# A pipeline over the routed part's tiles, and a slot table of row numbers, in a graph layer with a mixture of experts

## The chip, the cores and the metric

The kernel runs on one core of a Trainium2 chip. The metric is the device time of one execution in microseconds; lower is better. Three runs of the kernel before took 1408.47, 1411.64 and 1416.46 us, median 1411.64. All other times here come from one profiled execution. Its span, from the first to the last instruction, is 1334.0 us.

## The reference, cut to what matters

```python
# x: 3125 nodes x 256; 50000 edges; D = 256, F = 1024, E = 8 experts, K = 2 of them for each node
x = x + gnn(layernorm(x), ...)        # gather h[src], weights from edge features, segment sum over dst
xn = layernorm(x)
shared = gelu(xn @ W1s + b1s) @ W2s + b2s
topw, topi = top_k(softmax(xn @ Wr), 2); topw = topw / sum(topw)
# routed, for each node n and each of its two experts e, with its weight w:
routed[n] += w * (gelu(xn[n] @ W1p[e] + b1p[e]) @ W2p[e] + b2p[e])
x = x + shared + routed
```

All is fp32. Products are made from halves: an operand is rounded to a high part, the remainder is the low part, and three matmuls (high-high, high-low, low-high) stand for one.

## The kernel before, in words

The program is a chain of blocks; at the end of each all engines meet.

*Node and edge blocks* (0 to 684 us). The edge block goes through 98 steps of 512 edges. GpSimd gathers the rows `h[src]` by four indirect DMAs a step (line 552), VectorE makes the edge products, TensorE sums them by one-hot matrices. On the side SP fills a table `slots_d` in HBM with blank rows of 258 words (line 522): 256 features, a node number and a weight.

*Update block* (684 to 779 us). It finishes the nodes, writes the new rows `xnew_d`, their layernorm `xn_d` and its columns `xT_d` to HBM, and computes the router's logits.

*Shared block* (779 to 924 us). Five groups of 640 nodes go through the shared expert. A group is 16 half blocks "up" (6 matmuls of 320 columns each, then Gelu on ScalarE, `hhi` on ScalarE, `hlo` on VectorE) and five "down" of 24 matmuls. During group 0 VectorE computes the routing: each node has two places (`pos_i`) in the slot table, where every expert owns whole tiles of 256 slots, three at least. `counts_i` holds each expert's number of tiles and its first tile. Then GpSimd writes rows to the table: SP loads the normalized rows of a group twice (line 1371), GpSimd puts node number and weight beside them and scatters 128 rows of 1032 bytes at a time (line 1448), 50 scatters. SP waits for these buffers in the same queue in which it loads the columns of the next group and stores the output.

*Routed block* (924 to 1334 us). Expert after expert, tile after tile; here there are 29 tiles. A tile s goes so:

- SP loads the tile's 256 rows of the slot table to `x_slot_tile` (line 1713) once VectorE has taken the node numbers and weights of the tile before (`meta_done`).
- TensorE turns them (`turn`, line 1871) into `psX`, in the middle of the down blocks of the tile before. ScalarE copies them to `xf`, VectorE makes `xhi` and `xlo` (lines 1802, 1804).
- TensorE does eight up blocks (`q_psA`, line 1293: 6 matmuls of 256 columns), ScalarE the Gelu (line 1763), VectorE `high` and `low` (lines 1811, 1815).
- TensorE then does eight down blocks (`q_psB`, line 1300: two halves of 3 matmuls), each waiting for its `hlo`.
- VectorE's output, after all its `low` of the tile: for each half of 128 slots the node number to `index`, `biased` (line 1834), `ob` (line 1837). It waits for `ob_free`.
- GpSimd adds `ob` to the rows of the output by an indirect DMA that adds (line 1739), waits until it has landed, frees `ob`, and only then issues the next: two additions a tile.

`index` and `ob` have one buffer for each half. Weights of the next expert are split into high and low parts in eight pieces of 512 columns (ScalarE line 1785, VectorE line 1852) during the first two tiles of an expert, four in each, and then SP loads the two matrices of a later expert (1024 KB each, lines 1259 and 1261) to `x_raw`. The experts are three times two in a loop and two behind it; tiles beyond an expert's second are a loop of their own (`further`).

## Time and profile before

| | |
|---|---|
| median of three runs | 1411.64 us |
| span of the profiled execution | 1334.0 us |
| its own time | the page gives none beside the span; the median above is 77.6 us more than the span |
| TensorE busy | 1217.9 us, 91% |
| VectorE busy | 1029.3 us, 77% |
| ScalarE busy | 826.6 us, 62% |
| GpSimd busy | 720.3 us, 54% |
| mean granted TensorE clock | 0.955 |

The page names engines so: PE is TensorE's matmuls, PEld its weight loads, DVE is VectorE, ACT ScalarE, POOL GpSimd, SP SyncE; a "q" behind the name is the engine's queue of other instructions. Times are from the span's start. The granted clock is 1.00 at the full 2.4 GHz. Matmuls overlap in the record, so that their rate is read from one start to the next. The busy share of a whole execution mixes stages with different limits: VectorE and TensorE are both nearly full in the edge stage, while in the routed stage VectorE works 254 of 410 us.

### The profile page before, as it was taken

What the parts mean: (1) busy time and instruction counts of PE and PEld (TensorE: products, weight loads), DVE (VectorE), ACT (ScalarE), POOL (GpSimd) and SP (SyncE); (2) the same over time, 40 slices, a digit from 0 to 9 for tenths busy, and PEclk for the clock granted to TensorE, in tenths of its full rate; (3) what the DMA queues carried; (4) which work ended last, traced back from release to release, by engine and by line L of the source; (5) the groups of instructions that cost most, each with busy time, mean ns of one, the idle gap of its engine ahead of it and who ended that gap; (6) DMA issues with size and microseconds to landing.
All of it is one profiled execution on the core that took longest, in us unless ns stands there. A gap on an engine that the chain in (4) does not pass through costs nothing. (4 is left out here: it accounts for less than half of the span.)

```text
span 1334.0 us, 32063 instructions
## 1 busy us (share of the span) xinstructions
PE 1217.9 (91%) x8631; PEld 1120.6 (84%) x8632; DVE 1029.3 (77%) x2584; ACT 826.6 (62%) x2362; POOL 720.3 (54%) x823
## 2 busy tenths in 40 slices
PE   2789999999999999999989899998998997989995
PEld 2578888888888888888887679998998997989995
DVE  7589999999999999999856866444765674666663
ACT  2688888888888888888834674453442443343431
POOL 7178888788887888878731104651242232233332
PEclk9989999999999999999975979999999998999998
DMA  6443444344344444434543474764324334332232
GB/s 241 155 131 111 120 117 119 111 119 120 111 122 120 115 116 118 121 110 118 171 126 116 163 259 131 251 216 140 99 44 103 78 62 99 95 95 46 46 49 28
DMA packets 107219, 160.47 MB, mean 120 GB/s; under 512 B 16414, under 2 KB 82750, under 8 KB 106656
## 3 DMA queue, kind: packets, MB, share of 16 engines
q1 hardware_dynamic: 73680, 90.86, 21.4%
q0 software_dynamic: 29568, 65.62, 20.6%
q10 hardware_dynamic: 3920, 3.41, 0.8%
q8 instruction: 19, 0.31, 0.1%
q14 instruction: 32, 0.26, 0.1%
HBM read 110.99 MB, written 48.85 MB: 120 GB/s over the span
## 5 line engine op out<-in xcount | busy, mean ns | idle before, releaser
L576 ACT ACTIVATE hots<-hot,sh_st 128x128 f32<-128x128 f32 x1568 | 467.9, 390 | 3.8 <-PE psY L743 3.3
L552 POOL DMA_INDIRECT rows<-h_tab,src_st x392 | 404.9, 1033 | 117.2 <-issue 116.9
L743 PEld LDWEIGHTS psY<-prod,hots 128*128 128x128 f32 x2352 | 324.6, 192 | 20.4
L743 PE MATMUL psY<-prod,hots 128*128 128x128 f32 x2352 | 326.1, 275 | 0.0
L1739 POOL DMA_INDIRECT out_rows<-q_ob,q_index x58 | 125.5, 2163 | 294.4 <-DVE q_ob L1837 193.3
L740 PE MATMUL psY<-prod,hots 128*128 128x256 f32 x784 | 234.4, 381 | 0.6 <-DVE prod L636 0.6
L636 DVE TENSOR_TENSOR prod<-psW,rows 128x384 f32<-128x384 f32 x392 | 213.8, 545 | 0.0
L1763 ACT ACTIVATE q_hf<-q_psA,q_b 128x256 f32<-128x256 f32 x232 | 109.7, 473 | 111.7 <-PE q_psA L1293 109.0
L1300 PE MATMUL q_psB<-x_whi,q_hhi 128*128 128x256 f32 x464 | 138.7, 299 | 24.5 <-DVE q_hlo L1815 24.5
L651 DVE TENSOR_TENSOR y_sb<-y_sb,psY 64x512 f32 x196 | 133.4, 681 | 10.2 <-issue 5.7
L1293 PE MATMUL q_psA<-q_xhi,x_whi 128*128 128x256 f32 x464 | 133.2, 287 | 4.0 <-DVE q_xlo L1804 2.8
L1300 PE MATMUL q_psB<-x_wlo,q_hhi 128*128 128x256 f32 x464 | 133.7, 288 | 0.0
L1300 PE MATMUL q_psB<-x_whi,q_hlo 128*128 128x256 f32 x464 | 133.7, 288 | 0.0
L1293 PE MATMUL q_psA<-q_xlo,x_whi 128*128 128x256 f32 x464 | 131.5, 283 | 0.0
L1293 PE MATMUL q_psA<-q_xhi,x_wlo 128*128 128x256 f32 x464 | 131.5, 283 | 0.0
L728 PE MATMUL psW<-w1hi,cols_hi 128*128 128x256 f32 x392 | 108.2, 309 | 16.2 <-DVE cols_hi L621 6.5
L740 PEld LDWEIGHTS psY<-prod,hots 128*128 128x128 f32 x784 | 119.4, 191 | 0.8 <-DVE prod L636 0.8
L634 DVE TENSOR_TENSOR prod<-psW,rows 128x128 f32<-128x128 f32 x392 | 110.5, 282 | 5.4 <-DMA rows<-h_tab,src_st 1.8
L1300 PEld LDWEIGHTS q_psB<-x_whi,q_hhi 128*128 128x128 f32 x464 | 90.6, 195 | 28.0 <-issue 27.0
L566 ACT ACTIVATE hid<-psE 128x512 f32<-128x512 f32 x98 | 58.7, 598 | 89.2 <-PE psE L720 87.6
L728 PEld LDWEIGHTS psW<-w1hi,cols_hi 128*128 128x128 f32 x392 | 75.0, 191 | 45.8 <-issue 45.1
L729 PE MATMUL psW<-w1lo,cols_hi 128*128 128x256 f32 x392 | 98.0, 283 | 0.0
(213 smaller groups left out, 2509.6 us busy)
## 6 DMA issues: line engine op xcount, KB each, us to landing
x_raw<-in_w SPq DMA_DIRECT2D x18, 1024.0 KB, 8.0
slots_d<-blank SPq DMA_DIRECT2D x49, 258.0 KB
x_slot_tile<-slots_d SPq DMA_DIRECT2D x30, 258.0 KB, 2.8
s_row<-xn_d SPq DMA_DIRECT2D x50, 128.0 KB, 3.1
cols_lo<-ele_split SPq DMA_DIRECT2D x196, 32.0 KB
rows<-h_tab,src_st POOLq DMA_INDIRECT x392, 2.8
x_sb<-in_x SPq DMA_DIRECT2D x5, 640.0 KB, 5.8
h_tab<-x_sb ACTq DMA_DIRECT2D x5, 640.0 KB, 3.3
```

Of the source, the lines that this page charges most:

```text
L552: pool.indirect_dma_start(out=rows[p][:, c, :, :].rearrange("p a u -> p (a u)"), out_offset=None, in_=h_tab, in_offset=bass.IndirectOffset ...
L576: ins = nc.scalar.activation(hots[p][:, 4 * c + k, :], hot[p][:, c, :], ACT.Copy, scale=sh_st[p][:, 4 * c + k:4 * c + k + 1])
L634: nc.vector.tensor_tensor(slots[:, 0::7, :], w[:, 0:2, :], rows[p][:, c, 0:1, :].to_broadcast([P, 2, MUL]), ALU.mult)
L636: nc.vector.tensor_tensor(slots[:, 1:7, :].rearrange("p (b k) u -> p b k u", b=2), w[:, 2:4, :].unsqueeze(2).to_broadcast([P, 2, 3, MUL]), ...
L651: ins = nc.vector.tensor_tensor(acc, acc, psY[p][lo:lo + HALF, :], ALU.add)
L728: nc.tensor.matmul(o, hidT[p][:, P * c:P * c + P], w1hi[:], start=True, stop=False)
L740: ins = nc.tensor.matmul(y[:, 1::2, :], hots[p][:, 4 * c, :], a[:, 4:8, :], start=(c == 0), stop=(c == C - 1), skip_group_check=True)
L743: ins = nc.tensor.matmul(y[:, 2 * k::6 - 2 * k, :][:, 0:2, :], hots[p][:, 4 * c + k + 1, :], a[:, 0::k + 1, :][:, 0:2, :], start=False, st ...
L1293: ins = nc.tensor.matmul(ps, w1_part(w, k, f), x(k), start=(n == 0), stop=(n == len(terms) - 1))
L1300: ins = nc.tensor.matmul(ps, h, w2_part(w, f), start=(f == 0 and n == 0), stop=(f == FC - 1 and n == 2))
L1739: pool.indirect_dma_start(out=out, out_offset=bass.IndirectOffsetOnAxis(ap=index[m][:], axis=0), in_=ob[m][:], in_offset=None, compute_op= ...
L1763: nc.scalar.activation(hf[f][:], psA[f % 4][:, 0:TOK], ACT.Gelu, bias=b1_st[:, f:f + 1]).then_inc(gelu_done, 1)
```

## The change

- *Slot table.* It holds only node number and weight (8 bytes), 94 places for each partition, so that one DMA loads all of it to SBUF (`meta_all`). It is blanked by one DMA; the 49 of the edge loop go. `place` gives the positions in that layout and works on both experts at once.
- *Shared block.* No row loads. The 50 scatters write `meta_i` straight to the table, and each waits (`turn_of`) for an up or down block of TensorE in groups 1 to 4. After the last GpSimd waits for all, loads the table and gathers the rows of tile 0 from `xn_d`.
- *Rows of a tile* are now gathered by GpSimd (`gather_rows`: two index copies, two indirect DMAs of 128 rows), into one buffer, as soon as TensorE has turned the tile before.
- *TensorE* interleaves the down blocks of tile s-1 with the up blocks of tile s: down f, up f; the transpositions of s+1 follow up block 1. A tile's down has one of two sides of `psB`, `xhi` and `xlo` have two sides. ScalarE writes `xhi` from PSUM; `xf` and VectorE's cast are gone.
- *VectorE's output* in tile s is that of tile s-2, after the first `low`; `xlo` of s+1 follows the third. *GpSimd* in one loop: rows of tile d+4, free `ob` half 1 of tile d-1 when its addition has landed, addition of half 0 of tile d, wait for it, addition of half 1.
- *Weights.* W1 and W2 of an expert are split in separate tiles (W2 in its own first tile, W1 of the next expert in the second) and loaded apart. The loop over experts is written out; copies of the biases are gone.

```diff
+def gather_rows(nc, pool, v, s):
+    for m in range(SUB):
+        ins = pool.tensor_copy(index[:, m:m + 1], meta_all[:, at(s), m, 0:1].rearrange("p o c -> p (o c)"))
+    ins.then_inc(v["index_set"], 1)
+    pool.wait_ge(v["index_set"], s + 1)
+    pool.sem_inc(v["gather_go"], 1)
+    for m in range(SUB):
+        pool.indirect_dma_start(
+            out=rows[:, m, :], out_offset=None, in_=v["xn_d"],
+            in_offset=bass.IndirectOffsetOnAxis(ap=index[:, m:m + 1], axis=0)).then_inc(v["rows_in"], 16)
...
+            def turn_of(n):
+                g, r = 1 + n // (FC + GROUP), n % (FC + GROUP)
+                if r <= FC:
+                    pool.wait_ge(up_done, g * UP + min(2 * r + 1, UP))
+                else:
+                    pool.wait_ge(down_done, g * GROUP + r - FC + GROUP)
...
+            for t in range(NT):
+                g = t // GROUP
+                if t % GROUP == 0 and g > 1:
+                    pool.wait_ge(sent[g % 2], 32 * GROUP * (g // 2))
+                for k in range(2):
+                    turn_of(2 * t + k)
+                    pool.sem_inc(send_go, 1)
+                    pool.indirect_dma_start(
+                        out=slots_d, out_offset=bass.IndirectOffsetOnAxis(ap=pos_i[:, t, k:k + 1], axis=0),
+                        in_=meta_i[:, t, k, :], in_offset=None).then_inc(sent[g % 2], 16)
+            pool.wait_ge(sent[0], 32 * GROUP * ((NG + 1) // 2))
+            pool.wait_ge(sent[1], 32 * GROUP * (NG // 2))
+            pool.dma_start(meta_all[:].rearrange("p n m c -> p (n m) c"), slots_d.rearrange("(p n) c -> p n c", p=P)
+                           ).then_inc(meta_in, 16)
+            pool.wait_ge(meta_in, 16)
+            gather_rows(nc, pool, v, 0)
...
+            pool.sem_inc(ob_free, 3 * SUB)
+            def rows_of(s):
+                pool.wait_ge(turned, s)
+                gather_rows(nc, pool, v, s)
...
+            with pool.Fori(1, all_but_two) as d:
+                rows_of(within(d + 4, TILES + 1))
+                landed(d - 1, 1)
+                add(d, 0)
+                landed(d, 0)
+                add(d, 1)
...
+            def output(s, e):
+                side = dve.snap(s % 2)
+                done = within(s - 2)
+                dve.wait_ge(ob_free, s * SUB + SUB)
+                dve.wait_ge(down_done, s + 1)
+                for m in range(SUB):
+                    nc.vector.tensor_copy(index[m][:], meta_all[:, at(done), m, 0:1].rearrange("p o c -> p (o c)"))
+                    nc.vector.tensor_tensor(biased[:, m, :], psB[:, at(side), m, :].rearrange("p o f -> p (o f)"),
+                                            b2_sb[:, e + 1, :], ALU.add).then_inc(biased_done, 1)
+                for m in range(SUB):
+                    dve.wait_ge(biased_done, s * SUB + m + 1)
+                    nc.vector.tensor_scalar(ob[m][:], biased[:, m, :],
                                            meta_all[:, at(done), m, 1:2].rearrange("p o c -> p (o c)").bitcast(F32),
                                            None, ALU.mult).then_inc(ob_done, 1)
...
+            def tile(s, e, done=None, after=None):
+                high(s, 0)
+                for f in range(FC):
+                    if f + 1 < FC:
+                        high(s, f + 1)
+                    low(s, f)
+                    if f == 0 and done is not None:
+                        output(*done)
+                    if f == 2:
+                        split_x(s + 1)
+                    if after is not None and f < HALF_W:
+                        after(f)
...
+            def tile(s, e, done=None, fresh=False):
+                for f in range(FC):
+                    if done is not None:
+                        down(*done, f, done_side, fresh)
+                    if f == 0:
+                        pe.wait_ge(xlo_done, s + 2)
+                    pe.wait_ge(gelu_done, s * FC + f + 1)
+                    up_product(nc, psA[f % 4][:, 0:TOK], whi[1 - h], wlo[1 - h],
+                               lambda k: xhi[:, at(side), k, :].rearrange("p o n -> p (o n)"),
+                               lambda k: xlo[:, at(side), k, :].rearrange("p o n -> p (o n)"), f).then_inc(up_done, 1)
+                    if f == 1:
+                        turn(s + 1)
```

## Rows read from the trace of the kernel before

**Rows 1.** Windows of the shared and routed parts: window, its us, busy us (instructions), clock, DMA share, GB/s.

```profile
779.00:924.00 145.00, 142.38 (x1084) 141.83 (x1084) 78.41 (x194) 77.42 (x169) 62.94 (x127) 0.98 0.61 193
924.00:1334.00 410.00, 363.46 (x2904) 355.63 (x2904) 253.70 (x793) 154.39 (x326) 125.45 (x58) 0.96 0.34 75
```

**Rows 2.** Chain of waits, an undisturbed routed tile: start, us, what.

```profile
1280.02 0.44 PE q_psX L1871 x4
...
1283.34 5.63 PE q_psA L1293 x48
...
1291.85 0.44 PE q_psX L1871 x4
```

**Rows 3.** Chain of waits, start of the routed part.

```profile
926.40 0.64 PE q_psX L1871 x4
...
928.99 8.62 PE q_psA L1293 x48
```

**Rows 4.** Timeline, the last rows of the span.

```profile
1324.99 1.55 POOL L1739 DMA_INDIRECT out_rows<-q_ob,q_index  x1 [3.26 <-DMA out_rows<-q_ob,q_index]
```

**Rows 5.** TensorE's waits from 915 us: us in total, times, longest.

```profile
PE q_psB L1300 <- DVE q_hlo L1815: 24.5, 11, 4.8
PE q_psX L1871 <- PEq L1310: 3.1, 1, 3.1
```

**Rows 6.** TensorE's timeline behind a gap.

```profile
1016.61 0.40 PE L1300 MATMUL q_psB<-x_whi,q_hhi 128*128 128x256 f32 x1 [4.23 <-DVE q_hlo L1815]
1016.82 0.39 PE L1300 MATMUL q_psB<-x_wlo,q_hhi 128*128 128x256 f32 x1
```

**Rows 7.** Chain of waits, two additions of one tile.

```profile
961.54 4.12 DMA out_rows<-q_ob,q_index
...
966.61 3.72 DMA out_rows<-q_ob,q_index
```

**Rows 8.** All additions: ns min/median/max of the issue, then issue to landing.

```profile
L1739 POOL DMA_INDIRECT out_rows<-q_ob,q_index x58: 1549/1551/6337, 945.2 to 1325.0; - x58
...
DMA to landing us min/median/max: 3.7/4.0/10.0
```

**Rows 9.** The scatters to the slot table, issue to landing.

```profile
DMA to landing us min/median/max: 2.4/2.9/6.9
```

**Rows 10.** VectorE's timeline, the output of one half.

```profile
1110.75 0.15 DVE L1833 COPY q_index<-q_meta 128x1 int32<-128x1 int32 x1 [7.18 <-POOLq L1743]
1110.82 0.41 DVE L1834 TENSOR_TENSOR q_biased<-q_psB,q_b 128x256 f32<-128x256 f32 x1
1111.27 0.35 DVE L1837 TENSOR_SCALAR q_ob<-q_biased,q_meta 128x256 f32<-128x256 f32 x1
```

**Rows 11.** GpSimd's timeline, a second and a first addition.

```profile
1085.44 6.00 POOL L1739 DMA_INDIRECT out_rows<-q_ob,q_index  x1 [3.58 <-DMA out_rows<-q_ob,q_index]
...
1112.42 1.55 POOL L1739 DMA_INDIRECT out_rows<-q_ob,q_index  x1 [8.15 <-DVE q_ob L1837]
```

**Rows 12.** GpSimd's timeline in the edge stage: index copy and gathers.

```profile
401.35 0.27 POOL L543 COPY src_st<-src_sb 128x4 int32 x1
...
402.44 1.30 POOL L552 DMA_INDIRECT rows<-h_tab,src_st  x1 [0.21 <-issue]
404.05 0.94 POOL L552 DMA_INDIRECT rows<-h_tab,src_st  x1 [0.30 <-issue]
```

**Rows 13.** VectorE's timeline, a dense run in an expert's first tile.

```profile
1086.46 0.28 DVE L1811 CAST q_hhi<-q_hf 128x256 fp32r<-128x256 f32 x1
...
1087.53 0.68 DVE L1852 TENSOR_TENSOR x_wlo<-x_raw,x_whi 128x512 fp32r<-128x512 f32 x1
1088.14 0.28 DVE L1811 CAST q_hhi<-q_hf 128x256 fp32r<-128x256 f32 x1
...
1090.06 0.69 DVE L1804 TENSOR_TENSOR q_xlo<-q_xf,q_xhi 128x512 fp32r<-128x512 f32 x1
```

**Rows 14.** Groups of instructions: the weight pieces on VectorE, busy us and mean ns.

```profile
L1852 DVE TENSOR_TENSOR x_wlo<-x_raw,x_whi 128x512 fp32r<-128x512 f32 x56 | 38.1, 681 | 0.0
```

More of the change, by code:

```diff
@@ L1327, in shared_block @@
         ob = sb("s_ob", [P, GROUP, FEAT])
-        row = [[sb(f"s_row{j}{k}", [P, ROW]) for k in range(2)] for j in range(GROUP)]
-        pos_st = [sb(f"s_pos{j}", [P, 2], I32) for j in range(GROUP)]
         TALL = [P, NT, EXPERTS]
@@ L1666, in routed_block @@
         block = ctx.enter_context(nc.Block())
[L1671 to L1682 removed]
+        HALF_W = PIECES // 2
@@ L1684, in further, with within, extent @@
+        def within(value, most=TILES - 1):
+            return nc.s_assert_within(value, 0, most, skip_runtime_bounds_check_because=
+                                      "the experts' tiles add up to TILES at most")
+        def extent(eng, e):
+            n = eng.value_load(counts_i[0:1, e:e + 1], min_val=LEAST, max_val=TILES)
+            first = eng.value_load(counts_i[0:1, EXPERTS + e:EXPERTS + e + 1], min_val=LEAST * e, max_val=TILES - LEAST)
+            return n, first
         def further(eng, n, first, tile):
@@ L1686, in further @@
             with eng.Fori(2, n) as i:
-                tile(nc.s_assert_within(first + i, 0, TILES - 1, skip_runtime_bounds_check_because=
-                                        "the experts' tiles add up to TILES at most"))
-        def second(first):
-            return nc.s_assert_within(first + 1, 0, TILES - 1, skip_runtime_bounds_check_because=
-                                      "every expert has its first two tiles")
-        def splits_next(e):
-            return not (isinstance(e, int) and e == EXPERTS - 1)
@@ L1745, in expert, with add @@
-            def expert(e, h, n, first):
-                tile(first)
-                tile(second(first))
-                further(pool, n, first, tile)
-            experts(pool, expert)
+            pool.sem_inc(ob_free, 3 * SUB)
+            def add(d, m):
+                pool.wait_ge(ob_done, d * SUB + m + 1 + 2 * SUB)
+                pool.sem_inc(add_go, 1)
+                pool.indirect_dma_start(
+                    out=out, out_offset=bass.IndirectOffsetOnAxis(ap=index[m][:], axis=0),
+                    in_=ob[m][:], in_offset=None, compute_op=ALU.add).then_inc(added, 16)
@@ L1789, in expert @@
                 act.sem_inc(begun, 1)
-                further(act, n, first, tile)
-            experts(act, expert)
+                further(act, n, first, lambda s, e=e: tile(s, e))
         @block.vector
@@ new lines, in tile, with split_w2, split_w1 @@
+                    if f == 2:
+                        split_x(s + 1)
+                    if after is not None and f < HALF_W:
+                        after(f)
+            split_x(0)
+            for e in range(EXPERTS):
+                n, first = extent(dve, e)
+                def split_w2(i, e=e):
+                    dve.wait_ge(w2_hi, (e - 1) * HALF_W + i + 1)
+                    w = (e + 1) % 2
+                    nc.vector.tensor_tensor(piece(wlo[w], 1, i), piece(raw, 1, i), piece(whi[w], 1, i).bitcast(F32),
+                                            ALU.subtract).then_inc(w2_lo, 1)
+                def split_w1(i, e=e):
+                    dve.wait_ge(w1_hi, e * HALF_W + i + 1)
+                    w = e % 2
+                    nc.vector.tensor_tensor(piece(wlo[w], 0, i), piece(raw, 0, i), piece(whi[w], 0, i).bitcast(F32),
+                                            ALU.subtract).then_inc(w1_lo, 1)
+                tile(first, e, (first, e - 1) if e > 0 else None, split_w2 if e > 0 else None)
+                tile(within(first + 1), e, (within(first + 1), e - 1) if e > 0 else None,
+                     split_w1 if e + 1 < EXPERTS else None)
@@ L1905, in _, with down @@
-            experts(pe, expert)
+            def down(s, e, f, side, fresh=False):
+                h = e % 2
+                if fresh and f % 2 == 0:
+                    pe.wait_ge(w2_lo, (e - 1) * HALF_W + f // 2 + 1)
+                    pe.sem_inc(begun, 1)
+                pe.wait_ge(hlo_done, s * FC + f + 1 + FC)
+                if f == 0:
+                    pe.wait_ge(ob_done, s * SUB + SUB)
+                for m in range(SUB):
+                    for k, (a, w) in enumerate(((hhi, whi[1 - h]), (hhi, wlo[1 - h]), (hlo, whi[1 - h]))):
+                        ins = nc.tensor.matmul(psB[:, at(side), m, :].rearrange("p o f -> p (o f)"),
+                                               a[:, f, P * m:P * m + P], w2_part(w, f),
+                                               start=(f == 0 and m == 0 and k == 0), stop=(f == FC - 1 and k == 2),
+                                               skip_group_check=True)
+                if f == FC - 1:
+                    ins.then_inc(down_done, 1)
@@ new lines, in _ @@
+            pe.sem_inc(down_done, 2)
+            turn(0)
+            for e in range(EXPERTS):
+                n, first = extent(pe, e)
+                if e > 0:
+                    pe.wait_ge(w1_lo, e * HALF_W)
+                    pe.sem_inc(begun, 1)
+                tile(first, e, (within(first - 1), e - 1) if e > 0 else None)
+                tile(within(first + 1), e, (first, e), e > 0)
+                further(pe, n, first, lambda s, e=e: tile(s, e, (within(s - 1), e)))
+            last = within(first + n - 1)
@@ L1909 @@
+            side = pe.snap(last % 2)
+            for f in range(FC):
+                down(last, EXPERTS - 1, f, side)
 def kernel(**inputs):
```

337 lines of the change are left out of this document (132 added, 205 removed).

## The prediction

> **What bounds the kernel now.** I read the slices, then the stages, the chain of waits, TensorE's waits, and the timelines of GpSimd and VectorE. The stages [rows 1] show TensorE busy 142.4 of 145.0 us in the shared part: little to win. In the routed part it is busy 363.5 of 410.0 us. An undisturbed tile there takes 11.83 us from one transposition of rows to the next [rows 2]: 0.44 for the transpositions, 2.88 for half of the down blocks (up to 1283.34), 5.63 for the up blocks, 2.88 for the other half. The first up block starts at 928.99 [rows 3]; TensorE's last down ends at about 1318.5, just before the last addition to the output, whose final issue starts at 1324.99 [rows 4]. That is 389.5 us for 29 tiles (464 down matmuls of a kind, 16 a tile), while 29 x 11.83 = 343.1. The 46 us between them are what a pipeline could give. 24.5 us are waits for `hlo` at the first down block [rows 5]; the rest is mostly slow clock behind them, at the lower of TensorE's two levels (1.2 in place of 2.4 GHz): after a gap of 4.23 us matmuls start 0.21 us apart [rows 6] where 48 of them take 5.63 in an undisturbed tile, 0.12 each.
>
> Why `hlo` is late: VectorE waits for `ob` to come free, hence for GpSimd's additions, which go one at a time. An addition takes 4.12 us from issue to landing, the next one starts 0.95 us after that [rows 7]. With x_raw loading it took up to 10.0 [rows 8].
>
> **The change, part by part.**
>
> *Edge stage.* 49 blank writes of 258 KB leave SP's queue, three small ones come. VectorE and TensorE are busy there, no wait of theirs names these writes: 0, bounds -3 to 0 us.
>
> *Shared part.* Fifty loads of 128 KB go, so the columns no longer stand behind them on SP: 0 to -1 us. `place` gets about 1.3 us of small VectorE work, beside TensorE's up blocks: 0. The 50 scatters now carry 8 bytes a row, each held until an up or down block. By the code the last waits for the second down of the last group; three downs, about 8.3 us (3 x 24 matmuls at 0.115), are left then; today TensorE ends at 926.40 less the 3.1 us of its wait [rows 3, 5], so that point is 915. Behind it on GpSimd stand the landing of that scatter (2.9 [rows 9]), a table load, two copies and two gathers. The load has no row; I take a scatter's 2.9 for it, bounds 2 to 7. Last scatter issued at 915, landed 918, table 921, gathers 924, landed about 926; today's first transposition is at 926.40 [rows 3]. So 0, bounds -1 to +5. One cast less before the first up: -0.4. First up at 928.6.
>
> *Routed part, TensorE.* Down of tile s-1 is interleaved with up of tile s. Same matmuls, so 11.83 us a tile. Tile 0 has only its up, at the slow clock as today: 8.62 [rows 3]. Tile 1 begins at 937.2, tile 2 at 949.0.
>
> *Routed part, GpSimd.* Here is the new bound, I think. One `ob` pair still serves every tile, and GpSimd, in order, now gathers rows too. In tile s VectorE's output waits until GpSimd has (a) seen the transposition of s+1, (b) gathered the rows of s+2, (c) freed `ob`. Behind the output come two additions in a row, and then GpSimd may gather again. That is a closed loop. Its steps, with u the moment VectorE begins the output:
> - output until the first `ob` is ready: 0.87 in today's order [rows 10], plus the second sum (0.41) now standing before it: 1.27
> - semaphore and issue overhead to the first addition: `ob` ready 1111.62 [rows 10], start 1112.42 [rows 11]: 0.80
> - landing 4.0 [rows 8], to the next start 0.95, issue 1.55: 6.50
> - index copies and two gathers: 0.27 + 0.21 + 0.95 + 0.30 + 0.95 = 2.7 [rows 12]
> - branch, and `ob` free to VectorE: 0.2 + 0.3
>
> Sum 11.8 us, against TensorE's 11.83. The landing of the second addition hides beside the gathers. Nothing is left over; I take 12.0, bounds 11.3 to 13.
>
> *In tiles that split weights the loop is longer.* An addition issued into a dense run of VectorE does not finish: at 1085.44 it took 6.00 us [rows 11] and ended 0.69 after VectorE's last instruction of that run, at 1090.75 [rows 13]. Twelve of 29 second additions took over 2.7 us so, those of the first and second tiles of an expert above all. After the change a dense run starts at u + 1.65 (both `ob` made): 6 pairs at 0.54 and one `hlo` 0.35, `xlo` 0.65, four weight pieces at 0.60 [rows 13], then the first three operations of the next tile 0.8: it ends at u + 9.1 with pieces, u + 6.7 to 7.1 without. The second addition starts at 1.27 + 0.80 + 4.95 = u + 7.0. Without pieces it gets through; with them it ends at 9.1 + 0.7 = 9.8 in place of 8.6: +1.2, bounds 0 to +3. I take 13.0. The pieces are 56 [rows 14], four a tile, so 14 tiles have them; 13 lie in tiles 2 to 27, as do 13 without. Half the weight load at a time also falls on gathers and the hidden landing instead of on an awaited addition: 0, bounds 0 to +2 for a load.
>
> *Sum.* In tile 2 the output can start at two down and two up blocks (2.84), the transposition 0.44, and 3.1 of GpSimd: u = 949.0 + 6.4 = 955.4. 26 loops: 13 x 12.0 + 13 x 13.0 = 325, so 1280.4 for tile 28. Then two outputs without gathers, 11.2 each (7.0 + 4.0 + 0.2), and 11.0 to the last landing: 33.4, so 1313.8. Today the last landing is 1324.99 + 4.0 = 1329.0 and the span ends 5.0 later; the same 5.0 gives a span of 1318.8 against 1334.0, so -15.2 us. The median of 1411.64 lies 77.6 us above the profiled execution's span; the page gives no time of its own for that execution, and I hold what lies outside the span as it is: 1396.4, say 1396 us. The mean loop is 12.5 us where a tile takes 13.4 today (389.5 / 29); the pipeline's own drain takes part of that back.
>
> *The page against the row.* A second addition is held by VectorE [rows 11, 13]; beside it a first addition takes 1.55, and all 29 first additions took at most 1.8 us, in spite of casts starting within 0.5 us. The Trainium skill, "SBUF — State Buffer", section "SBUF: two separate sides", says that VectorE in a two-port mode locks GpSimd out so that it "cannot write the descriptors". The second additions agree, the first ones speak against taking it for every issue. It is rival C.
>
> **Rivals.**
>
> A. *GpSimd's loop is shorter than TensorE's tile.* For: the sum is 11.8, and where TensorE falls behind, GpSimd catches up. Then 26 x 11.83 = 307.6 replaces 325: 17.4 less, 1379 us.
>
> B. *The loop is one us longer (the other side).* The place is the two additions and the gathers that stand in one queue now. A first addition lands in 5 instead of 4 us behind 256 gathered rows, or a second is held for 3 us and more, as in [rows 11], or copies and branch take more than the edge stage shows. 28 loops x 1 = +28: 1424 us. It decides from 15.2 / 28 = 0.54 us a loop, a mean of 13.04. For: knife-edge sum, and waits beyond 4 us cost the clock as well [rows 6]. Against: queued rows have mostly landed when the addition is issued 2.1 us later.
>
> C. *First additions are locked out too.* Issued at u + 2.1, they would be held through the dense run: to 7.8 instead of 3.6 without pieces, to 9.8 with them (where the second addition then goes free), so loops of 16.2 and 18.0: +120 us, 1516. If they slip through while VectorE computes `xlo` from PSUM, +0.6 in 13 loops only: 1404. For: the held second additions [rows 11]; against: 29 of 29 first additions.
>
> D. *The change doesn't pipeline:* waits move from `hlo` to `xlo` and `ob`, with slow clock behind them, and nothing is gained: 1405 to 1419.
>
> **How the numbers follow.** Forecast 0.33 (its own range 1386 to 1405), A 0.25, B 0.25, C 0.07, D 0.10. A run of this kernel tells 0.5% (7 us) from no change. Below 1404.6: A, nearly all of the forecast: 0.57. Within 7 us: D and edges of forecast and B: 0.13. Above 1418.7: most of B, C, part of D: 0.30. The range goes from 1376 (A with 3 us from the edge stage) to 1426 (B), with C outside.
>
> **What would show it.** Right: TensorE's waits for `hlo` gone, small waits at the first up block for `xlo` in tiles with pieces; first additions 12 to 13 us apart; GpSimd waiting for no transposition after tile 3; VectorE's index copy waiting for GpSimd in each tile; the stretch from TensorE's last matmul to the end longer by about 15 us. A shows as GpSimd waiting for the transposition and tiles at 11.83. B or C: distances over 13 and first additions above 2 us, with the clock below 1.0. Wrong at the root: a first transposition much later than 926, or additions that land otherwise than in 4 us.

## The result, and the profile after

The changed kernel takes 1353.3 us (median of four runs, 1348.53 to 1359.1) against 1410.06 for the kernel before beside it (1406.63 to 1416.46): ratio 0.9633, 95% interval 0.9592 to 0.9673, so 56.8 us faster. Ratios, here and below, leave out a kernel's runs that lie more than 1.5% above its fastest. The forecast was 1396 with a range from 1376 to 1426. The sign was right, the time lies below the range. The profiled execution has a span of 1346.7 us and took 1348.53: a run is 1.8 us longer than its span, not 77.6.

The stages after, windows of the shared and the routed part (window, its us, busy us and instructions of PE, PEld, DVE, ACT, POOL, clock, DMA share, GB/s), which answer to [rows 1]:

```profile
810.00:959.60 149.60, 142.46 (x1084) 141.89 (x1085) 79.61 (x201) 76.51 (x169) 52.27 (x56) 0.98 0.35 109
959.60:1346.70 387.10, 349.71 (x2904) 346.02 (x2904) 226.67 (x724) 157.20 (x318) 190.50 (x178) 0.96 0.36 77
```

From the shared part's first matmul to the end are 536.7 us (1346.7 - 810.0); before they were 554.7 (1334.0 - 779.3). That is -18.0 where the forecast had -15.2. But the shared part starts 30.7 us *later* than in the profile shown of before, though the edge stage ahead of it is the same code but for the blank writes, and still the kernel is 56.8 us faster. So two things stand to be explained: the routed part, and what the profile shown of before doesn't hold.

TensorE's waits from 955 us, answering to [rows 5]:

```profile
PE q_psA L1311 <- DVE q_xlo L1805: 9.6, 11, 1.7
PE q_psX L1882 <- DVEq L1799: 6.0, 1, 6.0
```

The 24.5 us for `hlo` are gone, in their place stand short waits for `xlo`, as the forecast said. GpSimd's timeline (start, us, what, idle time before it and who ended it), one loop without weight pieces and the start of one with them, answers to [rows 11, 12]:

```profile
1090.05 1.98 POOL L1712 DMA_INDIRECT out_rows<-q_ob,q_index  x1 [1.71 <-DVE q_ob L1830]
1095.37 1.69 POOL L1712 DMA_INDIRECT out_rows<-q_ob,q_index  x1 [3.35 <-issue]
1096.51 0.88 POOL L1626 COPY x_slot_index<-x_meta_all 128x1 int32 x2
1098.26 1.02 POOL L1631 DMA_INDIRECT x_slot_rows<-xn_d,x_slot_index  x1 [0.86 <-POOL x_slot_index L1626]
1099.58 0.99 POOL L1631 DMA_INDIRECT x_slot_rows<-xn_d,x_slot_index  x1 [0.31 <-issue]
1101.81 3.19 POOL L1712 DMA_INDIRECT out_rows<-q_ob,q_index  x1 [1.24 <-DVE q_ob L1830]
1108.22 1.77 POOL L1712 DMA_INDIRECT out_rows<-q_ob,q_index  x1 [3.22 <-issue]
```

The loop from 1090.05 to 1101.81 is 11.76 us, the next one (to 1114.47) 12.66. From the first addition at 1002.29 to the one at 1312.49 there are 25 loops of 12.41 us on average; the forecast had 12.5. VectorE beside the held addition (same columns):

```profile
1101.13 0.69 DVE L1855 TENSOR_TENSOR x_wlo<-x_raw,x_whi 128x512 fp32r<-128x512 f32 x1
1101.73 0.29 DVE L1811 CAST q_hhi<-q_hf 128x256 fp32r<-128x256 f32 x1
...
1102.27 0.69 DVE L1855 TENSOR_TENSOR x_wlo<-x_raw,x_whi 128x512 fp32r<-128x512 f32 x1
...
1103.40 0.69 DVE L1805 TENSOR_TENSOR q_xlo<-q_psX,q_xhi 128x512 f32 x1
```

`q_xlo` reads PSUM. It ends at 1104.09, and the addition issued at 1101.81 ends at 1105.00, 0.91 later. Of the 26 first additions with a `q_xlo` beside them, 24 end 0.89 to 0.92 us after its end. That is 1.6 us after its start (0.69 + 0.91), as long as an issue takes with nothing in its way (1.55 us, [rows 11]), as if the held issue began with `q_xlo`. A tile with weight pieces has two pieces more ahead of `q_xlo`, so its first addition takes 3.2 us instead of 1.98.

### The profile page after: what moved, and what is told of

Same layout as the page of the kernel before. It is cut to its first block and busy times, and to the rows that moved or that the text cites. A ratio compares the mean times of both kernels' runs of the same rounds, so it can differ in the third digit from the quotient of the medians.

```text
span 1346.7 us, 31820 instructions
## 1 busy us (share of the span) xinstructions
PE 1220.2 (91%) x8631; PEld 1122.7 (83%) x8631; DVE 981.8 (73%) x2523; ACT 827.4 (61%) x2353; POOL 722.3 (54%) x873
## 5 line engine op out<-in xcount | busy, mean ns | idle before, releaser
L552 POOL DMA_INDIRECT rows<-h_tab,src_st x392 | 398.4, 1016 | 155.9 <-issue 154.7
L743 PEld LDWEIGHTS psY<-prod,hots 128*128 128x128 f32 x2352 | 334.7, 196 | 35.6 <-issue 13.4
L743 PE MATMUL psY<-prod,hots 128*128 128x128 f32 x2352 | 339.1, 279 | 11.1 <-issue 10.8
L740 PE MATMUL psY<-prod,hots 128*128 128x256 f32 x784 | 242.5, 392 | 4.0 <-DVE prod L636 2.7
L1767 ACT ACTIVATE q_hf<-q_psA,x_b 128x256 f32<-128x256 f32 x232 | 110.0, 476 | 193.6 <-PE q_psA L1311 188.7
L1712 POOL DMA_INDIRECT out_rows<-q_ob,q_index x58 | 119.9, 2067 | 138.4 <-issue 87.7
L1311 PE MATMUL q_psA<-q_xhi,x_whi 128*128 x464 | 132.5, 286 | 9.8 <-DVE q_xlo L1805 9.6
L1311 PE MATMUL q_psA<-q_xlo,x_whi 128*128 x464 | 131.3, 283 | 0.0
L1311 PE MATMUL q_psA<-q_xhi,x_wlo 128*128 x464 | 130.7, 282 | 0.0
L740 PEld LDWEIGHTS psY<-prod,hots 128*128 128x128 f32 x784 | 122.6, 196 | 7.2 <-DVE prod L636 5.7
L1311 PEld LDWEIGHTS q_psA<-q_xhi,x_whi 128*128 128x128 f32 x464 | 87.7, 189 | 12.6 <-issue 12.6
```

The source lines that it names most:

```text
L552: pool.indirect_dma_start(out=rows[p][:, c, :, :].rearrange("p a u -> p (a u)"), out_offset=None, in_=h_tab, in_offset=bass.IndirectOffset ...
L740: ins = nc.tensor.matmul(y[:, 1::2, :], hots[p][:, 4 * c, :], a[:, 4:8, :], start=(c == 0), stop=(c == C - 1), skip_group_check=True)
L743: ins = nc.tensor.matmul(y[:, 2 * k::6 - 2 * k, :][:, 0:2, :], hots[p][:, 4 * c + k + 1, :], a[:, 0::k + 1, :][:, 0:2, :], start=False, st ...
L1311: ins = nc.tensor.matmul(ps, w1_part(w, k, f), x(k), start=(n == 0), stop=(n == len(terms) - 1))
L1712: pool.indirect_dma_start(out=out, out_offset=bass.IndirectOffsetOnAxis(ap=index[m][:], axis=0), in_=ob[m][:], in_offset=None, compute_op= ...
L1767: nc.scalar.activation(hf[f][:], psA[f % 4][:, 0:TOK], ACT.Gelu, bias=b1_sb[:, e + 1, f:f + 1]).then_inc(gelu_done, 1)
```

## The experiments

Sixteen kernels ran in four sets; each set ran on one chip, with the kernel before beside it. The sets found it at four medians: 1326.8, 1405.7, 1426.0 and 1426.3 us. Within a set the runs of the kernel before lie within 3% of each other. I call the chip of the first set the quiet one, the other three disturbed. No chip was seen in two sets, so a property of the chip and its condition at that time can't be told apart, and why they differ, the runs don't tell. The result's 1410.06 is of the disturbed kind.

### First set: where are the 77.6 us? (quiet chip)

**c0**, the kernel before, unchanged.

> The kernel before, unchanged, with its own time beside its span. After the change a run takes 1.9 us more than its span; the profiled execution before had a span of 1334.0 us, 76 us under the median of its runs. Theory E (edge stage): the timed executions before spend those 76 us in the edge stage, which in the profile ended at 684 us: expected here an edge stage ending at 740 to 760 us, a span near 1405, own time 2 us above it. Rival O (outside): the span is 1334 again and the time 1410, so 70 us lie outside the span and the change removed them there.

Measured: 1329.5 us (10 runs, 1321.5 to 1337.5), profiled span 1332.2, its stages within 3 us of the profile shown of before. The time of every run is its span plus 1.8. So the profile shown of before is like a run of some 1335 us, and not like the runs of 1411 beside which it stood. Neither theory came as stated, since this chip has no run near 1410: nothing is lost outside the span, against rival O, and where a run of 1410 loses its time stays open until the third set.

**c1**, the changed kernel, unchanged.

> The changed kernel, unchanged, on the same chip as the others. Expected 1353 us (1348 to 1359), edge stage ending near 723 us, GpSimd's loop 12.4 us. It tells how much of the differences between profiles is scatter.

Measured: 1314.9 us (10 runs), and not 1353; the edge stage ends at 682 and not at 723. Profile against profile: 1332.2 to 1316.8, -15.4 us, where the forecast had -15.2. Medians: -14.6 against c0, -11.9 against the other 25 runs of the kernel before (1302 to 1340). The ratios are 1.0006 [0.9951, 1.0062] for c1 and 1.0072 [1.0026, 1.0118] for c0; by them the gain is 0.7%, 9 us. So on the quiet chip it is 9 to 15 us. Its stages:

```profile
781.10:928.90 147.80, 141.95 (x1084) 141.78 (x1085) 79.58 (x201) 76.81 (x169) 52.07 (x56) 0.97 0.35 110
928.90:1316.80 387.90, 351.36 (x2904) 347.99 (x2904) 226.75 (x724) 157.50 (x318) 190.14 (x178) 0.96 0.36 77
```

The shared part is 148.0 before (c0, 779.2 to 927.2) and 147.8 here; the routed part with the end 405.0 and 387.9, -17.1.

**e1**, the blank writes put back into the changed kernel, and **e2**, taken out of the kernel before.

```
 e1  sp.dma_start(v["aside_d"][at(first_slot, TOK), :]...,        # in the edge loop, 49 times
                  blank[:].unsqueeze(1).to_broadcast([P, SUB, FEAT])).then_inc(z_out, 16)
 e2 -sp.dma_start(slots_d[at(first_slot, TOK), :]..., blank...)   # in the edge loop
    +act.dma_start(slots_d.rearrange("(n p) f -> p n f", p=P), blank...)   # once, ahead of it
```

> The changed kernel, with the 49 blank writes of the edge loop put back on SP's queue (to a tensor of their own that nobody reads, 256 KB each). Theory E1 (the blank writes slow the edge stage): about 1353 + 57 + 15 = 1400 to 1425 us, the edge stage as long as before. Rival E2 (they cost nothing): 1353 us as the changed kernel.

> The kernel before, with the 49 blank writes taken out of the edge loop; one transfer on ScalarE's queue at the start of the edge stage writes the same 12.6 MB. Theory E1: 1410 less some 40 to 60 us, 1350 to 1370, with a few us lost in the first steps. Rival E2: 1410 or a little above.

Measured: e1 1307.3 us (ratio 0.9979 [0.9904, 1.0054]), e2 1333.0 (1.0116 [1.0017, 1.0214]). Here the writes cost nothing; e1 is even 8 us under c1, for which I have no cause (in the traces the shared part starts at 771.6 in e1 and at 781.1 in c1, and is followed by the same 535 us).

### Second set: the routed part's loop (disturbed chip)

**c2**, the changed kernel again.

> The changed kernel once more, unchanged, as the base for the others of this set. Theory S (the chip, or what it is doing, sets the edge stage): the kernel before and this one are either both near 1330 and 1315 us, with the edge stage ending near 683 us, or both 40 to 80 us later, with the whole difference ahead of the end of the edge stage. Rival (the difference lies in the routed part): shared part's first piece to the end would differ from 393.1 us (first trace after) and about 394 us by more than 5 us.

Measured: 1353.4 beside 1405.7 of the kernel before, ratio 0.9643 [0.9572, 0.9714]: the result again. Shared part's start to the end: 536.8 us, as in the first trace after, and 535.7 in c1. Theory S holds for the changed kernel: against c1 its 27 us are ahead of the shared part. In c2's edge stage ScalarE waits 69.8 us in 29 waits that the profile calls "remote", put down to no engine of the core (63.4 us in 26 of them up to 660 us); in c0, c1 and e1 there is none.

**r1**: copies and gathers after the second addition's landing.

```
-                rows_of(within(d + 4, TILES + 1))
                 landed(d - 1, 1)
+                rows_of(within(d + 4, TILES + 1))
                 add(d, 0)
```

> GpSimd's loop waits for the second addition's landing before it copies and gathers for the tile four on, instead of behind them. Loop theory (in tiles with weight pieces GpSimd's closed loop of output, addition, landing, addition, landing sets the period, and the copies and gathers already lie inside the second landing): the output is free earlier by nothing, and copies and gathers (4.05 us) come ahead of the first addition that waits for the output (0.85 after it), so the loop grows by up to 4.05 less the 1.27 + 0.85 us that the output takes, about 1.9 us in each of 26 loops: 20 to 50 us slower, 1335 to 1365 if the base is 1315. Rival (TensorE's 11.8 us is what bounds nearly all tiles and the loop is slack): within 5 us of the base. Rival 2 (the free signal was late because the copies and gathers stood ahead of it): faster by 5 to 15 us.

Measured: 1372.9 us, +19.5 on c2, just short of the 20 to 50; from the first turn to the end the traces have 411.3 us against 386.7, +24.6. GpSimd's timeline of r1:

```profile
1100.14 0.31 POOL L1626 COPY x_slot_index<-x_meta_all 128x1 int32 x2 [2.49 <-DMA out_rows<-q_ob,q_index]
1101.32 1.02 POOL L1631 DMA_INDIRECT x_slot_rows<-xn_d,x_slot_index  x1 [0.87 <-POOL x_slot_index L1626]
...
1103.94 1.63 POOL L1712 DMA_INDIRECT out_rows<-q_ob,q_index  x1 [0.30 <-issue]
```

Copies and gathers now stand between landing and addition, 3.8 us, and the output (about 1.3 + 0.8) runs beside them; the loop here is 12.8 (1091.14 to 1103.94), 13.3 on average over 25 loops. It is a closed loop on GpSimd that sets the tile.

**r3**: VectorE's weight pieces cut to 2 columns (the low parts of the experts' weights are left out).

```
-  nc.vector.tensor_tensor(piece(wlo[w], 1, i), piece(raw, 1, i), piece(whi[w], 1, i).bitcast(F32), ALU.subtract)
+  nc.vector.tensor_tensor(piece(wlo[w], 1, i)[:, 0:2], piece(raw, 1, i)[:, 0:2], ...)     # and for part 0
```

> VectorE's subtractions for the low parts of the routed experts' weights work on 2 columns of each piece instead of the whole piece; the low parts of those weights are left out of the result. Hold theory (the first addition's issue takes 3.2 us instead of 1.98 only because VectorE runs weight pieces back to back beside it): first additions all take under 2.1 us, the tiles with pieces fall from about 12.9 to 11.9, 12 to 20 us faster than the base. Rival (the longer issue is from something else, the landing rows or the copies ahead): first additions of 3.2 us stay in the same tiles, and the time is within 5 us of the base.

**r2**: two outputs and two sets of indices, by the tile's parity; GpSimd's loop unrolled by two for it.

```
-  ob = [sb(f"q_ob{m}", [P, FEAT]) for m in range(SUB)]
+  ob = sb("q_ob", [P, 2, SUB, FEAT])
-  pool.sem_inc(ob_free, 3 * SUB)
+  pool.sem_inc(ob_free, 4 * SUB)
```

> Two outputs and two sets of slot indices, by the tile's parity, so that VectorE's output of a tile no longer waits for the landing of the tile before; GpSimd's loop is unrolled by two for it. Loop theory: the output leaves the loop, GpSimd's own row of two additions and two landings plus issues is under 11.8 us, and every tile is at TensorE's 11.83: 26 loops at a mean of 12.4 become 11.85, 12 to 19 us faster than the base (1296 to 1303 if the base is 1315). Rival (the additions follow each other at their own 12.4, since each waits for the landing of the one before and is held by VectorE's weight pieces): within 4 us of the base. Rival 2 (additions held longer by VectorE's work beside them): slower.

Measured: r3 1341.3 us, -12.1 on c2; r2 1334.4, -19.0. From the first turn to the end the traces have 376.1 and 370.4 us against c2's 386.7, so -10.6 and -16.3; the rest of the medians lies ahead of it, where runs scatter by some us. All additions in the trace of r3 (ns min/median/max of the issue):

```profile
L1712 POOL DMA_INDIRECT out_rows<-q_ob,q_index x58: 1549/1670/2142, 998.1 to 1335.1; - x58
```

and in that of r2:

```profile
L1712 POOL DMA_INDIRECT out_rows<-q_ob,q_index x58: 1549/1626/1846, 990.6 to 1323.2; - x58
```

In the first trace after the longest takes 3202 ns, in c2 3279. With short pieces no addition is held over 2.15 us, and the loops are 11.87 on average: hold theory right, and its price is 11 to 12 us. With two outputs tiles are at 11.6 to 12.2 in spite of whole pieces, since VectorE's output comes when TensorE is done and not when GpSimd is. The chain of waits by line shows the loop leave the path: in c2

```profile
PE q_psA L1311 4%; DMA out_rows<-q_ob,q_index 4%; PE q_psB L1898 4%; DVE q_hhi L1811 1%; DVE q_hlo L1815 1%; POOL x_slot_rows L1631 1%; DVE q_xlo L1805 1%; POOL x_slot_index L1626 1%; DVE x_wlo L1855 0%; PE q_psX L1882 0%; DVE q_ob L1830 0%
```

and in r2

```profile
PE q_psA L1311 12%; PE q_psB L1901 12%; DMA out_rows<-q_ob,q_index 1%; PE q_psX L1885 1%; DMA x_slot_rows<-xn_d,x_slot_index 0%; POOL x_slot_rows L1631 0%; POOL out_rows L1712 0%; POOL x_slot_index L1626 0%; POOLq L1718 0%; POOLq L1710 0%; 
```

r2 beats both kernels: 0.9523 [0.9442, 0.9604] of the kernel before.

### Third set: the kernel before on a disturbed chip

**d0**, the kernel before; **d1**, the changed kernel with the blank writes (the edit of e1); **d2**, the kernel before without them (the edit of e2); **r4**, the edits of r2 and r3 together.

> The kernel before, unchanged, once more. Theory S (the chip sets the edge stage): if this set's kernel before is near 1405 us, its profile shows what the traces of the changed kernel at 1345 us show and those near 1317 us don't, that is ScalarE, VectorE waiting in the edge stage on nothing that the profile names as an engine of the core (26 waits, 63.4 us for ScalarE), and more of it than the 40 us of the changed kernel: edge stage ending near 755 us instead of 684, all else as in the profile shown. If near 1328 us, there are no such waits. Rival (the 75 us lie spread over the stages): shared part's start to the end more than 8 us longer than 553 us.

> The changed kernel with the 49 writes of 256 KB of the kernel before put back into the edge loop. Theory B (where the edge stage is disturbed, these writes cost it the other 35 to 40 us): in a set whose kernel before is near 1405 us, 30 to 40 us above the changed kernel's 1353, with the difference in the edge stage; in a set near 1328 us nothing, as measured there (1307 beside 1315). Rival (the writes cost nothing anywhere and the difference of the kernel before lies in its other lines): within 6 us of 1353.

> The kernel before without the writes in the edge loop (one transfer on ScalarE's queue in their place). Theory B: in a set whose kernel before is near 1405 us, 30 to 40 us faster than it (1365 to 1375), the edge stage ending near 720 us. Rival: within 6 us of 1405. In a set near 1328 us: within 6 us of it, as measured.

> Two outputs by the tile's parity and VectorE's short weight pieces together; the low parts of the routed experts' weights are left out of the result. Theory P (with two outputs every tile is at TensorE's own 11.83 us, so nothing that VectorE or GpSimd gives up can be seen): routed part within 3 us of the two-output version (first turn to last matmul 348.9 us), time within 4 us of it at the same state of the edge stage. Rival (the additions or VectorE still set some tiles): 4 to 10 us shorter.

Measured, with the kernel before at 1426.0: d0 1429.6, d1 1374.7 (0.9588 [0.9516, 0.966]), d2 1435.7 (1.0051 [1.0014, 1.0089]), r4 1355.6 (0.9534 [0.9467, 0.9601]). Theory B falls: the shared part starts at 836.5 (d0) and 836.7 (d1) with the writes, at 839.6 (d2) and 833.5 (r4) without them. Theory S was right on the edge stage (ScalarE has 47 "remote" waits of 105.1 us; the last addition to `y_sb` starts at 737, late but short of the forecast 755, against 683 on the quiet chip) and wrong that all else is as shown: its rival, a second place, came true. r4's first turn to its last matmul is 347.8 us beside 348.9 of r2: TensorE's own pace, theory P. Windows of d0, shared part and routed part with the end:

```profile
836.50:1020.30 183.80, 158.31 (x1085) 154.46 (x1086) 78.68 (x194) 76.07 (x169) 64.08 (x127) 0.89 0.48 153
1020.30:1427.40 407.10, 365.19 (x2904) 358.04 (x2904) 254.15 (x792) 154.44 (x326) 124.29 (x58) 0.94 0.33 75
```

and of d1, on the same chip:

```profile
836.70:986.60 149.90, 142.92 (x1085) 141.99 (x1085) 79.67 (x201) 76.52 (x169) 52.37 (x56) 0.98 0.35 109
986.60:1372.90 386.30, 349.41 (x2904) 345.81 (x2904) 226.51 (x724) 157.12 (x318) 189.88 (x178) 0.96 0.36 77
```

Here is the missing gain, on this chip: 33.9 us in the shared part and 20.8 in the routed part, 0.2 against it ahead of them, 54.5 together. The medians differ by 54.9. On the quiet chip the same shared part of the same kernel takes 148.0, with the same ten scatters 1.27 us apart five times over and no gap of TensorE above 2 us. What happens in it here ("issue" marks an engine that waited for nothing that the profile shows, "remote" one released by nothing that it can name): GpSimd's timeline of d0, first and last of ten scatters in a row,

```profile
893.85 0.96 POOL L1448 DMA_INDIRECT slots_d<-s_row,s_pos  x1
895.12 0.96 POOL L1448 DMA_INDIRECT slots_d<-s_row,s_pos  x1 [0.30 <-issue]
...
905.26 0.96 POOL L1448 DMA_INDIRECT slots_d<-s_row,s_pos  x1 [0.30 <-issue]
```

TensorE's,

```profile
901.80 0.28 PE L1300 MATMUL s_psB<-x_wlo,s_hhi 128*128 128x256 f32 x1
902.51 0.38 PE L1300 MATMUL s_psB<-x_whi,s_hlo 128*128 128x256 f32 x1 [0.43 <-issue]
903.92 0.28 PE L1300 MATMUL s_psB<-x_whi,s_hhi 128*128 128x256 f32 x1 [1.04 <-issue]
...
906.06 0.28 PE L1300 MATMUL s_psB<-x_whi,s_hlo 128*128 128x256 f32 x1 [1.73 <-issue]
907.47 0.37 PE L1300 MATMUL s_psB<-x_whi,s_hhi 128*128 128x256 f32 x1 [1.13 <-issue]
```

and VectorE's:

```profile
898.17 0.42 DVE L1524 TENSOR_TENSOR s_biased<-s_psB,x_b 128x256 f32<-128x256 f32 x1 [2.19 <-PE s_psB L1300]
...
908.34 0.42 DVE L1524 TENSOR_TENSOR s_biased<-s_psB,x_b 128x256 f32<-128x256 f32 x1 [9.29 <-remote]
```

TensorE goes on to 902 at 0.11 us a matmul and then gets one out in 1 to 2 us, waiting for nothing that the profile knows. The down block VectorE waits for, one of 24 matmuls, must have been through 2.8 us after the one before, near 901, yet VectorE starts at 908.34. All go on 2 us after the tenth scatter is issued (905.26 + 0.96 = 906.22). Behind the pause matmuls start 0.21 apart, the lower of TensorE's two levels, which is in the window's 0.89.

### Fourth set: number in a row, or size of the rows? (disturbed chip)

**f1**, the changed kernel with its 8-byte scatters in a row; **f2**, the kernel before with its 1032-byte scatters held to TensorE's blocks; **f3**, the changed kernel; **f4**, the changed kernel with two of a step's four gathers in the edge stage (half of the neighbour rows stay zero).

```
 f1 -                    turn_of(2 * t + k)
 f2 +                        n = 2 * j + k
    +                        if n <= FC:
    +                            pool.wait_ge(up_done, g * UP + min(2 * n + 1, UP))
    +                        else:
    +                            pool.wait_ge(down_done, g * GROUP + n - FC + GROUP)
 f4 -                        for c in range(C):
    +                        for c in range(0, C, 2):
                                 pool.indirect_dma_start(...).then_inc(row_in[p][c], 16)
    +                            pool.sem_inc(row_in[p][c + 1], 16)
```

> The changed kernel without the waits that hold each of GpSimd's 50 scatters back to a block of TensorE: they go out in a row. Theory G (on some chips a row of scatters without pause makes the other engines stand, whatever they carry): where the kernel before takes over 1400 us, the shared part (first matmul to first turn, 149.9 us in the changed kernel) grows by 15 to 40 us and the time with it; where it takes about 1328 us, nothing. Theory W (the 1032-byte rows did it, and the spacing does nothing): within 5 us of the changed kernel on every chip.

> The kernel before with each scatter of its shared part held to a block of TensorE in the same group (up pairs, then a down block), its 1032-byte rows as they were. Theory G: where the kernel before takes over 1400 us, its shared part falls from 183.8 to 150 to 160 us (the first group's ten scatters, whose blocks have passed, still go out in a row), 22 to 34 us faster. Theory W: within 6 us of the kernel before. On a chip where it takes about 1328 us: within 5 us either way.

> The changed kernel, unchanged, as the base of this set. Where the kernel before is over 1400 us: 0.955 to 0.965 of it, with waits in the edge stage that the profile puts down to none of the core's engines, and a shared part of 147 to 151 us. Where it is about 1328 us: 0.985 to 0.992 of it and no such waits.

> The changed kernel with two of the edge stage's four gathers of a step left out (two of the four columns of neighbour rows stay zero, so that part of the messages is left out). Theory G, extended to the edge stage (GpSimd's indirect transfers without pause are what disturbs it on some chips): where the kernel before is over 1400 us, the waits put down to no engine of the core fall to under a third and the edge stage ends 25 to 45 us earlier than in the changed kernel; about 1328 us: within 6 us of it, since GpSimd's 4 gathers (5.0 of 6.15 us a step) are hidden beside VectorE. Rival (something else, the instruction stream or the other cores, disturbs the edge stage): the waits stay and the edge stage ends within 8 us of the base.

Measured, with the kernel before at 1426.3: f3 1371.7 (0.961 [0.9539, 0.968]); f1 1438.7 (1.0089 [1.0041, 1.0136]), 67 us above f3; f2 1402.7 (0.9823 [0.9755, 0.9891]), 23.6 under the kernel before; f4 1282.2 (0.8986). The shared part of f1:

```profile
832.70:1040.80 208.10, 148.63 (x1085) 146.38 (x1086) 79.62 (x201) 77.08 (x169) 51.32 (x57) 0.84 0.24 73
```

of f3:

```profile
844.30:994.00 149.70, 142.82 (x1085) 141.95 (x1085) 79.62 (x201) 76.50 (x169) 52.15 (x56) 0.98 0.35 109
```

and of f2:

```profile
835.70:997.20 161.50, 149.40 (x1085) 147.26 (x1085) 78.71 (x194) 77.07 (x169) 60.88 (x127) 0.94 0.55 174
```

Theory G holds in both directions and theory W falls: spacing large rows takes 22.3 us out (161.5, against 183.8 in d0, which stood on another chip; the medians of this set alone say 23.6), small rows in a row put 58.4 in (208.1 against 149.7 on the same chip). f2 keeps 161.5 and not 150 to 160, and its trace shows why: not ten but the first twenty scatters still go out 1.27 us apart, with VectorE waiting 4.5 and 8.4 us for nothing that the profile can name; the thirty behind them, mostly 1.75 us apart, leave no such wait. f1 wasn't run on the quiet chip. I had allowed 40 for f1; fifty in a row disturb longer than five times ten. ScalarE's timeline of f1 shows it, its rows between the first scatter (868.84) and just after the last (931.12):

```profile
891.86 0.53 ACT L1470 ACTIVATE s_hf<-s_psA,x_b 128x320 f32<-128x320 f32 x1 [8.29 <-remote]
...
907.96 0.53 ACT L1470 ACTIVATE s_hf<-s_psA,x_b 128x320 f32<-128x320 f32 x1 [15.22 <-issue]
...
924.76 0.53 ACT L1470 ACTIVATE s_hf<-s_psA,x_b 128x320 f32<-128x320 f32 x1 [15.91 <-remote]
```

with TensorE standing for up to 22.1 us at a time.

f4 bears on the edge stage. Waits of ScalarE there in f3 (us in total, times, longest):

```profile
ACT hid L566 <- remote: 89.6, 42, 9.8
ACT hid L566 <- PE psE L720: 53.3, 34, 4.6
```

and in f4, where no "remote" wait is left:

```profile
ACT hid L569 <- PE psE L723: 73.5, 97, 6.7
```

The edge stage ends at 665 instead of 747. That is 82 us, more than the 45 I allowed, and 18 below the quiet chip's 683, so part of it is not the disturbance. f4 halves the number of gathers and their bytes together, so it doesn't tell which of the two counts there. Its routed part has other data and one tile fewer (28), so only the edge stage is read from it.

## Why the prediction was right on the routed part and wrong on the time

**Edge stage, 0 (bounds -3 to 0): right.** e1 and e2 show no cost of the blank writes on the quiet chip. On a disturbed one the shared part starts at 836.5 and 836.7 with them (d0, d1), at 839.6 and 833.5 without (d2, r4), so they cost about 3 us at most.

**"I hold what lies outside the span as it is": this step failed.** The forecast was -15.2 us and -56.8 was measured; most of the 41.6 us between them come from it. Nothing lies outside the span but 1.8 us. The 77.6 us were a difference between executions: the profile I worked from was of the quiet kind, the median of the disturbed kind. Where such a difference lies is seen in d0 against c0, 95.2 us apart: 57.3 ahead of the shared part (836.5 against 779.2), 35.8 in the shared part (183.8 against 148.0) and 2.1 behind it. The first term is in both kernels and stayed; the second the change removed. For the result's own set this is inferred, since it holds no trace of the kernel before. If both kernels reach the shared part at the same time there, an estimate follows: 1353.3 - 1.8 - 536.7 = 814.8 for its start, and 1410.06 - 1.8 - 814.8 = 593.5 from there to the end of the kernel before. That is near d0's 590.9 and 40.5 above c0's 553.0.

**Shared part, 0: right for the profile, wrong for the runs.** It measured 147.8 against 148.0 on the quiet chip and 149.9 against 183.8 on a disturbed one. I had costed the scatters held until a block only for the wait they add (0 us) and not for the pause between them. f1 and f2 show that the pause is the gain, and not the 8 bytes. The first turn came at the predicted place on the quiet chip (928.9, forecast 926.4 with bounds of -1 to +5), though by another way: 5.9 to 6.0 us of its lateness are a wait for VectorE's queue, where it had 3.1 [rows 5]. The table load took 2.3 us in d1 (taken: 2.9).

**TensorE's tile, 11.83: right.** 11.80 to 11.91 in 14 of the 29 tiles of the first trace after.

**GpSimd's loop, 12.0 and 13.0, mean 12.5: right, 12.41.** Of its terms, copies and gathers were mis-sized: 4.06 (1096.51 to 1100.57) for 2.7, as the two copies beside VectorE take 0.88 and the first gather starts 0.86 behind it. It was made good by two overlaps: the copies start 0.55 before the recorded end of the second addition, and the output runs as soon as the second gather is taken up, so only 1.24 instead of 2.57 lie between the gathers' end and the next addition. 5.32 + 1.14 + 4.06 + 1.24 = 11.76; the forecast sum was 11.8.

**Hold in tiles with pieces, +1.2, bounds 0 to 3: the size right, the instruction wrong.** The first addition is held (3.19 against 1.98), not the second, and not to the end of the dense run but until `q_xlo`. This is the second branch of rival C ("slip through while VectorE computes `xlo` from PSUM"), which I had put at +0.6. r3 prices it at 10.6 us by the traces and 12.1 by the medians; the first trace after has 12 such additions, so 0.9 to 1.0 each. That 29 of 29 first additions were short in the kernel before did not carry over, and why isn't settled. 24 of them started behind VectorE's output and ahead of its next cast, where now they start among casts. But five started among casts then too (998.74, for one) and took only 1.60 to 1.77 us. The Trainium skill, "SBUF — State Buffer", section "SBUF: two separate sides", says that GpSimd can't write descriptors while VectorE runs in a two-port mode. The 24 of 26 ends at 0.89 to 0.92 us behind an operation that reads PSUM agree with it, and r3 does.

**Sum: right for the quiet chip, with some luck in the last digit.** -15.2 forecast; -15.4 from c0 to c1, but c1 reached the shared part 1.9 us later, and from there on it is -17.3 (553.0 to 535.7), and -18.0 in the first trace after. In c1, counted from the shared part's start, the first addition came 2.2 us later than forecast, the 26 loops took 4.0 less (321.0 for 325), and the rest 1.9 less. The drain, from TensorE's last matmul to the end, is 26.1 us where it was 15.5 (+10.6; forecast about 15).

**Rivals.** A needed GpSimd's loop to be shorter than TensorE's tile: only with a second output, in r2 and r4, are tiles at TensorE's pace. B and C's large case and D didn't come. One of B's grounds, that waits beyond 4 us cost the clock [rows 6], reads no limit out of the trace: the three such waits before (4.2 to 4.8 us) were followed by TensorE's lower level, but so was one of 1.9 us (at 1071.07). None of the rivals, and no bound, spoke of the kernel before being disturbed in a place the change removes; the gap between span and median was the sign of it, and it went into the sum as a constant.

**Open.** What is disturbed. The pauses hit TensorE, ScalarE and VectorE at once and not GpSimd. It is hardly instruction loading: the Trainium skill, "Runtime: NRT & Kernel Launch", section "Instruction fetch mechanics", says that each sequencer fetches its instructions over a DMA queue of its own, but in f3 the instruction queues moved 3 packets between 80 and 747 us, where ScalarE has 42 "remote" waits. All runs, the timed ones too, come with a span, so their instructions were recorded; whether a run that records nothing would pause as well, these runs can't say. Nor do they say why one chip of four is free of it.

## What to carry to other kernels

When a profile's span and the timed runs differ by more than the 1.8 us seen here, take a profile of a run that has the timed length, and find in which stage the difference lies before you sum, since a change may remove just that. Long rows of indirect transfers from GpSimd, one each 1.27 us, made TensorE, ScalarE and VectorE stand on the disturbed chips, while rows of ten passed on the quiet one; held each behind a block of TensorE, mostly 1.75 us apart or more, they did not, and on the quiet chip that cost nothing (147.8 against 148.0). In a loop closed over output, additions and landings a second output buffer gained 19.0 us (r2), and copies and gathers moved behind the landing lost 19.5 (r1).

## What the runs showed of the hardware that I had not expected

- The same kernel took 1326.8 us on one chip and 1405.7 to 1426.3 on three others, each within 3% over one set.
- Ten scatters in a row (12.4 us) all but stopped TensorE for 6 us and VectorE for 9; fifty (63 us) cost 58 us, though their rows carried 8 bytes and not 1032. This was on disturbed chips.
- With half the gathers the edge stage ends 82 us earlier on a disturbed chip, without one such wait.
- An addition that VectorE held got through 0.9 us behind the end of `q_xlo`, which reads PSUM (24 of 26 first additions).
